# Order of a rotary loop's matrix work, its query casts, and the place of half a top-eight search in a hybrid layer stack

## The reference

```python
# rotary attention, 16 heads of 8 channels
q = q * cos + _rotate_half(q) * sin
k = k * cos + _rotate_half(k) * sin
q = _rms_norm(q, q_norm_w)
k = _rms_norm(k, k_norm_w)
scores = jnp.einsum('bhtd,bhsd->bhts', q, k) / jnp.sqrt(jnp.float32(D))
scores = jnp.where(causal[None, None], -jnp.inf, scores)
att = jax.nn.softmax(scores, axis=-1)
y = jnp.einsum('bhts,bhsd->bhtd', att, v)
...
# product keys: 8 heads, 32 x 32 experts, the best 8 of each head
s1, i1 = jax.lax.top_k(sim1, K)
s2, i2 = jax.lax.top_k(sim2, K)
all_sc = (s1[..., :, None] + s2[..., None, :]).reshape(b, t, H, K * K)
fs, pk = jax.lax.top_k(all_sc, K)
hidden = jax.nn.gelu(jnp.einsum('btd,bthkd->bthk', xn, wd), approximate=False)
hidden = hidden * jax.nn.relu(fs)
return jnp.einsum('bthk,bthkd->btd', hidden, wu)
```

## Time and profile before

| what | value |
|---|---|
| median of 3 runs | 2643.84 us (2643.37 to 2650.24) |
| the profiled execution's own time | 2650.11 us |
| its span, first to last instruction | 2648.4 us |
| mean granted TensorE clock | 0.937 of full speed |
| busy share of the span: PE, DVE, ACT, POOL | 79%, 85%, 70%, 63% |

### The profile page before, as it was taken

One profiled execution on the slowest core, in us unless ns is written; L12 is line 12 of the kernel. 1 busy time (PEld: TensorE's weight loads), 2 busy tenths in 40 slices (PEclk: granted clock), 3 DMA queues, 4 the chain that ended last, 5 costly groups with the idle time before them and its releaser, 6 DMA issues. The chain is left out here.

```text
span 2648.4 us, 59121 instructions
## 1 busy us (share of the span) xinstructions
PE 2094.3 (79%) x17450; PEld 1742.0 (66%) x17451; DVE 2243.9 (85%) x5522; ACT 1860.2 (70%) x4274; POOL 1661.6 (63%) x1495
## 2 busy tenths in 40 slices
PE   7578888888699999783588877888888448888888
PEld 3266666667588887573466656777777237777777
DVE  7699999864788887648788858999999779999998
ACT  4789999565555555553355548999998349999997
POOL 2679999447000000565555539999999119999997
PEclk9799999999899999896699989999999769999999
DMA  2023333141100000120100000000000000000000
GB/s 49 3 90 97 96 97 97 58 142 51 49 1 0 0 0 9 55 58 22 41 2 0 0 1 1 0 0 0 0 0 0 0 1 1 8 4 4 4 4 9
DMA packets 67623, 69.84 MB, mean 26 GB/s; under 512 B 10248, under 2 KB 46304, under 8 KB 67488
## 3 DMA queue, kind: packets, MB, share of 16 engines
q1 hardware_dynamic: 59408, 56.33, 7.2%
q0 software_dynamic: 4992, 10.23, 1.4%
q10 hardware_dynamic: 3088, 1.62, 0.2%
HBM read 56.50 MB, written 11.67 MB: 26 GB/s over the span
## 5 line engine op out<-in xcount | busy, mean ns | idle before, releaser
L1965 POOL TENSOR_TENSOR k5a_psums<-k5a_sims 128x1024 f32<-128x1024 f32 x224 | 421.8, 1917 | 16.0 <-DVE k5a_w L2173 11.8
L1965 POOL TENSOR_TENSOR k7a_psums<-k7a_sims 128x1024 f32<-128x1024 f32 x224 | 421.7, 1917 | 14.3 <-DVE k7a_w L2173 9.1
L1060 POOL TENSOR_TENSOR mc_hc<-mc_h,mc_cs 128x512 f32<-128x512 f32 x256 | 327.7, 1296 | 32.1 <-DVE mc_h L1027 16.5
L2030 PE MATMUL k5a_pw<-g_ident,k5a_w 128*128 128x128 f32 x2048 | 265.4, 277 | 70.3 <-DVE k5a_hid L2181 45.9
L2030 PE MATMUL k7a_pw<-g_ident,k7a_w 128*128 128x128 f32 x2048 | 262.5, 277 | 69.7 <-DVE k7a_hid L2181 46.4
L2030 PEld LDWEIGHTS k5a_pw<-g_ident,k5a_w 128*128 128x128 f32 x2048 | 226.8, 141 | 113.5 <-DVE k5a_w L2173 52.6
L1027 DVE TENSOR_TENSOR_SCAN mc_h<-mc_dA,mc_inj 128x512 f32<-128x512 f32 x256 | 298.6, 1199 | 2.3 <-PE mc_inj L916 1.8
L2030 PEld LDWEIGHTS k7a_pw<-g_ident,k7a_w 128*128 128x128 f32 x2048 | 228.2, 142 | 108.4 <-issue 63.8
L2173 DVE SCALAR_TENSOR_TENSOR k7a_w<-k7a_psums,k7a_best,k7a_lift 128x1024 f32<-128x1024 f32 x224 | 279.4, 1272 | 0.5 <-ACT k7a_lift L2101 0.3
L2173 DVE SCALAR_TENSOR_TENSOR k5a_w<-k5a_psums,k5a_best,k5a_lift 128x1024 f32<-128x1024 f32 x224 | 279.0, 1269 | 0.5 <-ACT k5a_lift L2101 0.3
L2101 ACT ACTIVATE k7a_lift<-k7a_psums 128x1024 f32<-128x1024 f32 x224 | 229.2, 1023 | 38.0 <-DVE k7a_w L2173 32.8
(11 more groups left out here) (503 smaller groups left out, 5904.5 us busy)
## 6 DMA issues: line engine op xcount, KB each, us to landing
mc_cs<-c_rows SPq DMA_DIRECT2D x128, 256.0 KB, 3.1
e_w<-in_L_ffn_W_dram SPq DMA_DIRECT2D x16, 256.0 KB, 6.0
token_rows<-e_zn SPq DMA_DIRECT2D x16, 256.0 KB, 3.1
e_zn<-token_out SPq DMA_DIRECT2D x16, 256.0 KB, 5.0
out_dram<-g_X SPq DMA_DIRECT2D x7, 256.0 KB, 2.3
e_zs<-token_rows,e_token POOLq DMA_INDIRECT x78, 2.5
token_out<-e_ys,e_token POOLq DMA_INDIRECT x78, 2.3
g_X<-in_L_attn_a_x_dram SPq DMA_DIRECT2D x4, 256.0 KB, 5.1
```

The source lines that it names most:

```text
L1060: nc.gpsimd.tensor_tensor(hc[:, q % RH, :], h_[:, q % RB, :], cs[:, S % RC, :], ALU.mult).then_inc(outs, 1)
L1965: nc.gpsimd.tensor_tensor(psums[:, h - 1, :, :], rows_of(p, h), s2, ALU.add).then_inc(pooled, 1)
L2030: ins = nc.tensor.matmul(pw[:, j, :], w[:, h % WR, j * P:(j + 1) * P], env.ident[:, :], start=(h == 0 and j % 4 == 0), stop=(h == HD - 1 a ...
```

## The change

It has four parts. In the product-key layers, the sixteen instructions of `top8` for tile t+1 are cut into two calls of eight: heads 0 to 3 now stand behind weighing 0, ahead of `finish` of tile t-1; heads 4 to 7 stay behind weighing 1. In the rotary loop on TensorE, `shift` of step 0 now stands ahead of `mix` 2 of the block before, and `mix` 0 of step 5 stands ahead of `place_y`. The slots of QS and KS are numbered anew, so that VectorE's cast of the queries is three instructions a block, not five, with three, two and one copies; ScalarE's cast of the keys is four instead of three (the slots of the first key part are no longer next to each other). The six products of parts are the same.

```diff
                         weigh(t, p, 0)
+                        if not final:
+                            top8(t + 1, 1 - p, 0)
                         if not begun:
                             finish(t - 1, 1 - p)
                         weigh(t, p, 1)
                         if not final:
-                            top8(t + 1, 1 - p)
+                            top8(t + 1, 1 - p, 1)
...
-                        nc.scalar.copy(ks[:, :, 0:3, :], spread(k, 3)).then_inc(kcast, 1)
+                        nc.scalar.copy(ks[:, :, 0:2, :], spread(k, 2))
+                        nc.scalar.copy(ks[:, :, 5, :], heads(k)).then_inc(kcast, 1)
...
                 def step(w, seq):
+                    if seq(0):
+                        shift(*seq(0), w)
                     if w == 0 and seq(-1):
                         mix(*seq(-1), 2)
-                    if seq(0):
-                        shift(*seq(0), w)
...
+                    if w == 5 and seq(0):
+                        mix(*seq(0), 0)
                     if w == 5 and seq(-1):
                         place_y(*seq(-1))
-                    if w == 5 and seq(0):
-                        mix(*seq(0), 0)
...
-                        nc.vector.tensor_copy(qs[:, :, 0, :], q).then_inc(qcast, 1)
-                        nc.vector.tensor_copy(qs[:, :, 3:6:2, :], spread(q1, 2)).then_inc(qcast, 1)
+                        nc.vector.tensor_copy(qs[:, :, 0:5:2, :], spread(q1, 3)).then_inc(qcast, 1)
...
-                        nc.vector.tensor_copy(qs[:, :, 1, :], heads(rq[:, 0, :])).then_inc(qcast, 1)
-                        nc.vector.tensor_copy(qs[:, :, 4, :], heads(rq[:, 0, :])).then_inc(qcast, 1)
+                        nc.vector.tensor_copy(qs[:, :, 1:4:2, :], spread(rq[:, 0, :], 2)).then_inc(qcast, 1)
...
-                        nc.vector.tensor_copy(qs[:, :, 2, :], heads(rq[:, 1, :])).then_inc(qcast, 1)
+                        nc.vector.tensor_copy(qs[:, :, 5, :], heads(rq[:, 1, :])).then_inc(qcast, 1)
```

More of the change, by code:

```diff
@@ L2142, in _, with top8 @@
             def _(dve):
[L2143 to L2147, removed]
+                def top8(t, p, half):
+                    if half == 0:
+                        need(dve, crossed, t)
+                        hold(dve, s_in, t + 1)
+                    for h in range(half * HD // 2, (half + 1) * HD // 2):
                         for s in range(2):
                             ins = nc.vector.max(top[:, h, s, :], sims[:, p, h, s, :])
-                    ins.then_inc(topped, 1)
+                    if half:
+                        ins.then_inc(topped, 1)
                 def rank(t, p):
@@ L2193, in _ @@
                 dve.wait_ge(floored, 1)
-                top8(0, 0)
+                top8(0, 0, 0)
+                top8(0, 0, 1)
                 form(0, 0)
@@ L2542, in cast @@
                         hold(act, placed, 4 * (n - 1))
-                        nc.scalar.copy(ks[:, :, 0:3, :], spread(k, 3)).then_inc(kcast, 1)
+                        nc.scalar.copy(ks[:, :, 0:2, :], spread(k, 2))
+                        nc.scalar.copy(ks[:, :, 5, :], heads(k)).then_inc(kcast, 1)
                     if part == 1:
                         need(act, krest, 2 * n + 1)
-                        nc.scalar.copy(ks[:, :, 3:5, :], spread(rk[:, 0, :], 2)).then_inc(kcast, 1)
+                        nc.scalar.copy(ks[:, :, 2:4, :], spread(rk[:, 0, :], 2)).then_inc(kcast, 1)
                     if part == 2:
                         need(act, krest, 2 * n + 2)
-                        nc.scalar.copy(ks[:, :, 5, :], heads(rk[:, 1, :])).then_inc(kcast, 1)
+                        nc.scalar.copy(ks[:, :, 4, :], heads(rk[:, 1, :])).then_inc(kcast, 1)
                 def exponentials(n, p, w):
@@ L2608, in rest @@
                         nc.gpsimd.tensor_tensor(heads(rk[:, 0, :]), k, ks[:, :, 0, :], ALU.subtract).then_inc(krest, 1)
-                        pool.wait_ge(qcast, 5 * n + 2)
+                        pool.wait_ge(qcast, 3 * n + 1)
                         nc.gpsimd.tensor_tensor(heads(rq[:, 0, :]), q, qs[:, :, 0, :], ALU.subtract).then_inc(qrest, 1)
@@ L2613, in rest @@
                         pool.wait_ge(krest, 2 * n + 1)
-                        nc.gpsimd.tensor_tensor(heads(rk[:, 1, :]), heads(rk[:, 0, :]), ks[:, :, 3, :], ALU.subtract).then_inc(krest, 1)
-                        pool.wait_ge(qcast, 5 * n + 4)
+                        nc.gpsimd.tensor_tensor(heads(rk[:, 1, :]), heads(rk[:, 0, :]), ks[:, :, 2, :], ALU.subtract).then_inc(krest, 1)
+                        pool.wait_ge(qcast, 3 * n + 2)
                         pool.wait_ge(qrest, 2 * n + 1)
@@ L2649, in place @@
                     if g == 2:
-                        need(pe, qcast, 5 * n + 5)
+                        need(pe, qcast, 3 * n + 3)
                     if g == MAX_BANK:
@@ L2798, in cast @@
                 def cast(n, p, part):
-                    q = QQ[:, bass.ds(2 * n, 2), :].rearrange("p t (h d) -> p (t h) d", d=D)
                     qs = slots(QS, p)
```

## The result

The changed kernel took 2625.35 us (median; 2622.49 to 2629.66 in 4 runs) against 2644.22 (2643.37 to 2650.24, 4 runs) for the kernel before: ratio 0.9923, interval 0.9911 to 0.9935. Its profiled execution took 2629.66 with a span of 2627.9, which is 20.5 less than before. The forecast was 2620.8 in a range of 2609 to 2636; the time lies in the range and 4.6 above the forecast.

What follows compares the result with a forecast made beforehand. It took VectorE's own work to bound the product-key stages and a chain between engines the rotary loop. Gains of 14.1 (k7a), 3.9 (k5a) and 5 (rotary), 23.0 us, off 2643.84 gave 2620.8, range 2609 to 2636.

Steps and rivals of the forecast that it cites:

- The hole: k7a, VectorE ahead of `finish`: 0.51 us a tile of idle time that the moved searches would close; 0.17 in k5a.
- rival two: k7a: GpSimd becomes the bound and the stage gains only 10.2 us; 2624.7 in all, chance 0.12.
- The price of the split: Product-key stages, at `finish`: its semaphore waits behind eight short searches cost 0.04 us a tile, between nothing and 0.14.
- no clock term stands in the sum: All three stages: TensorE's granted clock is 0.98 to 1.00, its upper level, so nothing was counted for it.
- rival five: k5a and k7a: later `finish` (0.58 and 0.24 us) delays every tile if TensorE bounds the ring; 2663.4, chance 0.05.
- the ring: k7a tile cycle: `finish`, weighing 1, sixteen searches (1.50 us), weighing 2, some 9 us of TensorE, `finish` again.
- TensorE still waits for weighing 2: k7a: of TensorE's 0.70 us wait there, only 0.24 would be used up by the later `finish`.
- The collision taken off: Rotary loop: VectorE's new casts meeting GpSimd, half a longest collision, 0.23 us a block off the upper bound 0.52.
- Rival one: Rotary loop: VectorE does not bind and TensorE's 1.18 us a block is gained, 16.5 us; 2609.3, chance 0.08.
- some 0.5 us or more: Rotary loop, predicted sign: how long `turn_max` on TensorE would now wait for VectorE in a block.
- Rival three: Rotary loop: GpSimd holds all three casts a block, 0.47 us each, 12.5 us lost; 2638.3, chance 0.08.
- Rival four: Product-key stages: similarities come too late, VectorE waits at the moved searches, only the rotary 5 us remain; 2638.8, chance 0.05.

Runs made afterwards that it cites:

- hide_first: Changed kernel with eight TensorE matmuls (next tile's first hidden products) moved ahead of the first sum, into the wait for `finish`: 2617.11 us, 0.9891; second time 2622.8, 0.990.
- search_only: Changed kernel's split search with the rotary loop of the kernel before: 2632.1 us, 0.9938 of the kernel before.
- place_first: Changed kernel with `place_y` ahead of `mix` 0 again in the rotary loop: 2627.6 us, 0.9923 of the kernel before.
- casts_only: Changed kernel with TensorE's rotary order as before the change, so only the new casts stay of the rotary parts: 2627.71 us, 0.9932 of the kernel before.

## Why the prediction came out as it did

**k7a, 14.1 forecast, 15.2 measured: right.** The hole closed, the searches found their data, and GpSimd's wait of 0.34 a tile went to nothing without GpSimd becoming the bound, so rival two fell:

```profile
L1965 POOL TENSOR_TENSOR k7a_psums<-k7a_sims 128x1024 f32<-128x1024 f32 x224 | 421.7, 1946 | 2.7 <-ACT k7a_sims L2076 2.7
```

The price of the split that I took as 0.04 is not measurable: tiles are shorter by 0.52, the whole hole.

**k5a, 3.9 forecast, 0.9 measured: the step that failed** is "no clock term stands in the sum". It was read from the clock before the change, 1.00, and held to stay. `finish` comes later after TensorE's last sum by the 0.58 that rival five names (measured 2.05 − 1.49 = 0.56 in an undisturbed tile), and the text asked only whether that delays the ring, not what TensorE's longer idle does to its own clock. With the clock at 1.00 the same VectorE order gave 5.8 (`hide_first`), so the mechanism of the term was right, and its size 1.9 too small: the split cost nothing here either.

A second statement fell with it: "TensorE still waits for weighing 2". Its waits for weighings went from 22.9 us in 33 times to 1.9 in 3 in k5a, and from 22.0 in 31 to none in k7a. The prediction took off the 0.70 only the 0.24 by which `finish` is later; but eight of the sixteen searches ahead of weighing 2 are gone as well, and 0.70 − 0.75 leaves nothing. All of its idle time now stood in one piece before `finish`. That was the point from which rival five was to decide, and it did not: the ring kept slack in that piece. The condition was drawn wrongly, while the rival's place, TensorE behind a later `finish`, was where the loss came from. That the time fell into the range although this loss was not foreseen is in part luck: the term of k5a was 1.7 too small (5.6 without the slow tiles), and that covered a third of the 4.7 lost.

**Rotary, 5 forecast, 3.9 measured** (5.8 to 5.9 in the four profiles with the shorter block). The block gained 0.25, not 0.30. The casts gave 0.17 (0.14 forecast), the earlier turning 0.35 (0.38), together the 0.52 named as the upper bound. The collision taken off, 0.23, was a guess of nearly the right size, by luck, and in the wrong place: it falls on the small casts before `turn_max`, not on the query casts. It is moreover due to one of the four parts of the change, which the forecast credited with nothing of its own because VectorE ends the block. Rival one, TensorE's 1.18 a block, is out: `turn_max` waits for VectorE's last small cast.

```profile
1400.58 0.29 PE L2702 MATMUL r4a_work<-g_identb,r_nb 128*128 128x128 bf16 x2 [1.22 <-DVE r_nb L2849]
```

The 1.22 answers to "some 0.5 us or more". The wait of 0.43 between maxima is gone, as said. Rival three, all query casts held, is out by their medians (ns shortest, median, longest):

```profile
L2810 DVE CAST r_QS<-r_QQ x16: 547/551/665, 1285.1 to 1519.6; 128x768 bf16 x12, 128x768 bf16<-128x768 f32 x4
L2814 DVE CAST r_QS<-r4a_rq x16: 408/434/874, 1287.4 to 1522.6; 128x512 bf16<-128x512 f32 x16
L2817 DVE CAST r_QS<-r4a_rq x16: 282/336/475, 1289.0 to 1526.1; 128x256 bf16<-128x256 f32 x16
```

Rival four is out: no search waits. The misses, 3.0 us in k5a and 1.1 in the rotary loop, against 1.1 more in k7a, make 3.0 of the 4.6 by which the median was missed. The rest, 1.6, is less than one set of runs differs from another: the changed kernel gave 2625.35 and 2630.3 in two sets, against 2644.22 and 2647.73.

What stays open is why six of 30 like stretches in k5a cost the clock and the others not. The rows show the same 2.05 us before both kinds. The slow tiles come at regular distances, every fourth or fifth tile, in `search_only`, `place_first` and `casts_only` as well, so it is not chance; but no run shows what sets the distance.

## What to carry to other kernels

When work is moved ahead of an instruction that TensorE waits for, add up TensorE's idle before and after the move by stretches, not in total: the total hardly changed here, and one longer stretch a tile cost 4.7 of the 5.6 us that k5a had gained, until eight independent matmuls were put into the middle of it. Read the granted clock and the lengths of all tiles of a stage, not one tile: the loss sat in 6 of 30. And when the order on one engine is changed, look at which short instructions of VectorE the masks of GpSimd now fall on.

## What the runs showed of the hardware

The granted clock fell from 1.00 to 0.50 in a loop in which TensorE was busy 86% of the time, after idle stretches of about 2 us, and was back at 1.00 under 4 us later. In the kernel before, whose idle time in all was greater but cut in two, 1.49 and 0.70 us a tile, it fell once in the 60 tiles, after a stretch of 1.77 us. The Trainium skill's page "TensorE: Matmul & The Clock Gate", section "HAM oscillation — how this bites in real kernels", describes a kernel that loses the clock in every tile while it waits for a transfer; here the wait is for VectorE, and only some tiles lose it.

A row of sixteen searches cut into two of eight, with `finish` and its waits behind the first, cost no measurable time: 13.76 us is the former tile less its whole hole.
